# Three row norms of an attention block, moved from ScalarE to VectorE

## The reference

```python
def layer_norm(x, w, b):
    mu = mean(x); var = mean(square(x - mu))
    return (x - mu) * rsqrt(var + 1e-5) * w + b

# mod = silu(c) @ wmod, cut into sa, ca, ga, sb, cb, gb
h = _layernorm(x) * (1 + ca) + sa
# attention block on h
a  = layer_norm(h, ln1_w, ln1_b)               # the row norm "xa"
x1 = h + softmax_band(a @ Wq, a @ Wk) @ (a @ Wv) @ Wo + bo
n2 = layer_norm(x1, ln2_w, ln2_b)              # the row norm "nrm_b"
y  = x1 + gelu(n2 @ W1 + b1) @ W2 + b2
x2 = x + ga * y
h3 = _layernorm(x2) * (1 + cb) + sb            # its row norm is "nrm_c"
xr, xk = mixes of h3 with h3 of the token before
out = x2 + gb * sigmoid(xr @ W_r) * (square(relu(xk @ W_k)) @ W_v)
```

## Time and profile before

| | before |
|---|---|
| median of 3 runs | 622.71 us |
| lowest and highest | 622.13, 622.75 us |
| profiled execution, its span from first to last instruction | 620.5 us |
| median less that span | 2.2 us |
| mean granted TensorE clock | 0.989 of full |
| PE, DVE, ACT, POOL busy | 92%, 65%, 72%, 61% |
| chain of work that ended last | PE 50%, ACT 17%, DVE 15%, issue 7%, POOL 7% |
| read and written in HBM | 22.31 MB, 4.49 MB |

### The profile page before, as it was taken

The page is one execution under the profiler, slowest core; times in us unless marked ns, Lnnn a source line. Parts: engine busy times, 40 slices in busy tenths (PEclk is TensorE's granted clock), DMA queues, the critical chain, the costliest instruction groups (busy, mean ns, idle before and its releaser), DMA issues.

```text
span 620.5 us, 16499 instructions
## 1 busy us (share of the span) xinstructions
PE 567.8 (92%) x6528; PEld 444.8 (72%) x6528; DVE 403.2 (65%) x830; ACT 446.9 (72%) x745; POOL 380.3 (61%) x610
## 2 busy tenths in 40 slices
PE   5889988999898999999898989899999989999996
PEld 2668757777776777677667767677767768878785
DVE  4676746686464788576867686578867475375453
ACT  2527447499968777897879786987788798955542
POOL 4387324657937957675767678586657378943430
PEclk9989989899999999999999999999999999999999
DMA  5635423434503051351235132533134242110111
GB/s 176 246 103 133 124 77 78 112 75 116 137 18 101 25 139 52 97 143 56 69 90 153 60 87 76 146 93 89 52 80 112 70 116 52 54 46 26 34 44 35
DMA packets 46364, 55.74 MB, mean 90 GB/s; under 512 B 11643, under 2 KB 33469, under 8 KB 46286
## 3 DMA queue, kind: packets, MB, share of 16 engines
q1 hardware_dynamic: 44454, 53.81, 31.4%
q10 hardware_dynamic: 1832, 0.87, 0.6%
HBM read 22.31 MB, written 4.49 MB: 43 GB/s over the span
## 4 chain that ended last, share of the span: by engine, by line
PE 50%; ACT 17%; DVE 15%; issue 7%; POOL 7%; DMA 1%; SPq 1%; ACTq 1%; DVEq 0%; POOLq 0%
PE rest L486 4%; PE rest L498 4%; PE rest L447 3%; PE rest L449 3%; PE rest L448 3%; DVE nmax L1530 3%; PE quad L342 3%; ACT rest L1048 3%; PE rest L361 3%; PE rest L474 3%; PE rest L239 3%; PE quad L398 2%; ACT hid_hi L1058 2%; ACT p L997 2%; DVE hid_lo L1590 2%
## 5 line engine op out<-in xcount | busy, mean ns | idle before, releaser
L2174 POOL TENSOR_SCALAR_AFFINE_SELECT p<-p 128x448 f32<-128x448 f32 x64 | 41.5, 649 | 102.8 <-ACT p L997 80.5
L1530 DVE TENSOR_REDUCE nmax<-quad 128x8 f32<-128x1032 f32 x64 | 79.0, 1234 | 2.2
L430 PE MATMUL rest<-bt_hi,w_hi 128*128 128x256 f16 x256 | 70.2, 274 | 5.3 <-DVE hid_lo L1590 5.1
L997 ACT ACTIVATE p<-quad,scale_s 128x576 f32<-128x576 f32 (+1 forms) x77 | 62.3, 822 | 15.7 <-PE quad L342 15.4
L1048 ACT ACTIVATE rest<-rest,bias,scale_g 128x256 f32<-128x256 f32 x128 | 63.0, 532 | 11.2 <-PE rest L432 11.0
L447 PE MATMUL rest<-w_hi,hid_hi 128*128 128x256 f16 x256 | 69.9, 273 | 0.9 <-DVE hid_lo L1590 0.9
L432 PE MATMUL rest<-bt_hi,w_lo 128*128 128x256 f16 x256 | 69.8, 273 | 0.0
L431 PE MATMUL rest<-bt_lo,w_hi 128*128 128x256 f16 x256 | 69.8, 273 | 0.0
L449 PE MATMUL rest<-w_hi,hid_lo 128*128 128x256 f16 x256 | 69.8, 272 | 0.0
L448 PE MATMUL rest<-w_lo,hid_hi 128*128 128x256 f16 x256 | 69.8, 272 | 0.0
L1590 DVE SCALAR_TENSOR_TENSOR hid_lo<-rest,inv_f,hid_hi 128x512 f16<-128x512 f32 x64 | 46.8, 744 | 25.1 <-ACT hid_hi L1058 24.8
(11 more groups left out here) (239 smaller groups left out, 1531.9 us busy)
## 6 DMA issues: line engine op xcount, KB each, us to landing
k_st<-k_two SPq DMA_DIRECT2D x64, 128.0 KB, 2.5
v_blk<-vn SPq DMA_DIRECT2D x16, 512.0 KB, 6.4
q_st<-q_two SPq DMA_DIRECT2D x64, 64.0 KB, 2.6
k_st<-k_two SPq DMA_DIRECT2D x64, 64.0 KB, 2.0
rb<-den_rows SPq DMA_DIRECT2D x16, 256.0 KB
x<-x SPq DMA_DIRECT2D x16, 256.0 KB, 3.0
out<-x SPq DMA_DIRECT2D x16, 256.0 KB, 2.2
xa<-x SPq DMA_DIRECT2D x7, 512.0 KB, 4.8
```

Source lines behind the costliest of these rows:

```text
L430: e.matmul(dst, w1_hi[:, k, ms], bt_hi[:, k, :], start=(k == 0), stop=False)
L997: e.activation(p32[gp % SLOTS][:, c0:c0 + 2 * w].rearrange("p (n c) -> p n c", n=2), (rest if gp < APART else quad)[:, b0 % HQ:b0 % HQ + 2 ...
L1530: e.tensor_reduce(nmax[:, :, :, qt].rearrange("p a j -> p j a"), quad[:, :, 2 * QB - 2:2 * WIN].rearrange("p j (c a) -> p j a c", a=2), AX ...
```

## The change

The three norms are computed on VectorE as (x - mean) * rs, in one `tensor_scalar` per tile with mean and rs as per-row scalars. ScalarE's 96 activations (32 each for xa, nrm_b, nrm_c) go, and on GpSimd the two nb instructions of each `rstd_h`, `rstd_b`, `rstd_c` (80 in all) with the wait between them. As mean and variance are now read later, the next statistics of each kind also hold for the ve step of the ones before, ve_x holds for h2, and two waits of the start-up are added. In VectorE's list the norms stand where ScalarE ran them by the clock. The loops of the lists are written out with literal numbers; TensorE's and SyncE's instructions stay in their order.

```diff
-            def norm_a(n):                                  (ScalarE)
...
-                e.wait_ge(s_nbh, n + 1)
-                for t in range(NT):
-                    e.activation(xa[:, t, :], h[n % 3][:, t, :], ACT.Identity, bias=nb_h[:, t:t + 1],
-                                 scale=rs_h[:, t:t + 1]).then_inc(s_xa, 1)
...
             def stats_h(n):                                 (VectorE)
...
+                hold(e, s_hve, n)
                 stats(h[n % 3], st_h, mv_h, range(NT), s_hst, s_hmv, 4 * n)
+
+            def norm_a(n):
+                if not batch(n):
+                    return
+                e.wait_ge(s_hrs, n + 1)
+                for t in range(NT):
+                    e.tensor_scalar(xa[:, t, :], h[n % 3][:, t, :], mv_h[:, t, 0:1], rs_h[:, t:t + 1],
+                                    ALU.subtract, ALU.mult).then_inc(s_xa, 1)
...
+            def norm_b(i):
...
+                e.wait_ge(s_brs, i + 1)
+                hold(e, s_tr2, i)
+                for t in range(2):
+                    e.tensor_scalar(nrm_b[:, t, :], x1[:, 2 * (i % 2) + t, :], mv_b[:, t, 0:1], rs_b[:, t:t + 1],
+                                    ALU.subtract, ALU.mult).then_inc(s_n2, 1)
...
             def rstd_h(n):                                  (GpSimd; rstd_b and rstd_c likewise)
...
                 hold(e, s_xa, 4 * n)
-                e.tensor_scalar(nb_h[:, :], mv_h[:, :, 0], -1.0, None, ALU.mult)
                 e.tensor_scalar(ve_h[:, :], mv_h[:, :, 1], 1.0, EPS, ALU.mult, ALU.add).then_inc(s_hve, 1)
                 e.wait_ge(s_hve, n + 1)
                 e.tensor_tensor(rs_h[:, :], ve_h[:, :], mhalf[:, :], ALU.pow).then_inc(s_hrs, 1)
-                e.wait_ge(s_hrs, n + 1)
-                e.tensor_tensor(nb_h[:, :], nb_h[:, :], rs_h[:, :], ALU.mult).then_inc(s_nbh, 1)
```

More of the change, by code:

```diff
@@ L769, in _ @@
             transposes_d(1)
[L770 to L829, removed]
@@ new lines, in _ @@
+            values_b(1)
+            up(3, 0, 1)
+            maxima(7, 0)
+            up(3, 1, 2)
+            maxima(7, 1)
+            up(3, 2, 3)
+            up(3, 3, 4)
+            out_project(4)
+            maxima(7, 2)
+            down(3, 0)
+            scores(26, 2, 4)
+            transposes_d(2)
+            scores(27, 0, 2)
+            transposes_a(4)
+            down(3, 1)
+            maxima(7, 3)
+            keys(2)
+            scores(27, 2, 4)
+            max_rows(7)
+            project(8)
@@ new lines, in _ @@
+            up(5, 0, 1)
+            maxima(9, 0)
+            up(5, 1, 2)
+            maxima(9, 1)
+            up(5, 2, 3)
+            up(5, 3, 4)
+            out_project(6)
+            maxima(9, 2)
+            down(5, 0)
+            scores(34, 2, 4)
+            transposes_d(4)
+            scores(35, 0, 2)
+            transposes_a(5)
+            down(5, 1)
+            maxima(9, 3)
+            keys(4)
+            scores(35, 2, 4)
+            max_rows(9)
+            project(10)
+            context(8)
@@ new lines, in _ @@
+            maxima(11, 0)
+            up(7, 1, 2)
+            maxima(11, 1)
+            up(7, 2, 3)
+            up(7, 3, 4)
+            out_project(8)
+            maxima(11, 2)
+            down(7, 0)
+            scores(42, 2, 4)
+            transposes_d(6)
+            scores(43, 0, 2)
+            transposes_a(6)
+            down(7, 1)
+            maxima(11, 3)
+            keys(6)
+            scores(43, 2, 4)
+            max_rows(11)
+            project(12)
+            context(10)
@@ L1059, in high_f @@
                                  scale=inv_f[:, 1:2]).then_inc(s_hh, 1)
-            def norm_c(i):
-                if not half_batch(i):
-                    return
-                e.wait_ge(s_nbc, i + 1)
-                hold(e, s_tr3, i)
-                for t in range(2):
-                    e.activation(nrm_c[:, t, :], x2[:, 2 * (i % 2) + t, :], ACT.Identity, bias=nb_c[:, t:t + 1],
-                                 scale=rs_c[:, t:t + 1]).then_inc(s_n3, 1)
             def modulate(i):
@@ L1612, in residual_b, with norm_c @@
                 e.wait_ge(s_x2, i + 1)
+                hold(e, s_cve, i)
                 stats(x2, st_c, mv_c, range(2 * (i % 2), 2 * (i % 2) + 2), s_cst, s_cmv, 2 * i)
+            def norm_c(i):
+                if not half_batch(i):
+                    return
+                e.wait_ge(s_crs, i + 1)
+                hold(e, s_tr3, i)
+                for t in range(2):
+                    e.tensor_scalar(nrm_c[:, t, :], x2[:, 2 * (i % 2) + t, :], mv_c[:, t, 0:1], rs_c[:, t:t + 1],
+                                    ALU.subtract, ALU.mult).then_inc(s_n3, 1)
             def mix(i):
@@ L2008, in _ @@
             gated(8)
-            maxima(NU - 2, 2)
+            maxima(14, 2)
             output(8)
@@ L2556, in load_residual @@
                 hold(e, s_out, DMA * (i - 1))
+                if i == 0:
+                    hold(e, s_top, DMA)
                 if i == 1:
```

1579 lines of the change are left out of this document (1046 added, 533 removed).

## The result

The changed kernel takes 656.42 us (median of 4 runs, 655.05 to 657.33), beside 622.73 for the kernel before on the same chip. The ratio is 1.0539 with a 95% interval of 1.0519 to 1.0559: 33.7 us slower. The forecast was slower by 11.5, 634.2, in a range of 626.5 to 643. The sign was right, the size a third of what came.

What follows compares the result with a forecast made beforehand. TensorE was taken as the bound, waiting for VectorE and not ScalarE; 5.4 + 3.2 + 1.8 - 1.0 + 1.6 + 1.4 - 0.85 = +11.5 us made the span 632.0 and the time 634.2, range 626.5 to 643.

Steps and rivals of the forecast that it cites:

- the price of one: One norm on VectorE: 0.34 us, from the same operation reading PSUM; a group of two 0.7, of four 1.4.
- The port rival: Steady norm groups on VectorE collide with GpSimd over the shared port pair: some +8 us more, 642; chance 0.19.
- (a): Four xa norms between ct and the second hid_lo, four steady batches: all 1.36 us reach TensorE's out projection, +5.4.
- (b): nrm_c's norm between two hid_lo, five times: no slack before the scores that need nmax's banks, +3.2 us.
- (c): nrm_b's norm behind the four mixed, four times: 0.68 us each less 0.22 slack before the scores, +1.8.
- the groups at nothing: Each batch's other nrm_b and nrm_c, where VectorE idles before a predicated copy: 0, uncovered up to 0.7 us each.
- (d): ScalarE's relief ahead of the second hid_lo's gelu: TensorE waits less for x, 0.25 us per batch, -1.0 for four.
- (e): The first nrm_b now stands behind k_two on VectorE, so TensorE's transposes start 1.6 us later: +1.6.
- (f): xa of batch 3, directly ahead of the predicated copy whose nmax TensorE awaits: +1.4 us; other early groups 0.
- (g): The tail: the last norm's bare chain gets shorter without the two nb steps, -0.85 us; the one before gains nothing.

Runs made afterwards that it cites:

- e10: Changed kernel with all norms left out but those of the first batch and half batch, and two unread nb_b steps back on GpSimd: 623.1 us.
- e3: Changed kernel with xa and nrm_b back on ScalarE with their nb steps, only nrm_c on VectorE: 629.2 us, ratio 1.011.
- e1: Changed kernel with nrm_b and nrm_c back on ScalarE with their nb steps, only xa's norm on VectorE: 636.2 us, ratio 1.021.
- e2: Changed kernel with xa and nrm_c back on ScalarE with their nb steps, only nrm_b on VectorE: 635.5 us, ratio 1.021.
- e12: Kernel before, with only the odd half batches' nrm_b moved to VectorE: 630.5 us, ratio 1.011.
- e9: Changed kernel with the two nb_b steps put back on GpSimd, their result unread: 652.0 us, ratio 1.046.
- e11: Changed kernel with each norm also writing a row sum (accum_out) and two unread nb_b steps back on GpSimd; output no longer the norm: 642.5 us.
- e7: Kernel before, with only the last two half batches' nrm_c (4 norms) moved to VectorE: 622.4 us, ratio 0.999.
- e13: Only xa's norms on VectorE, in batches 4 to 7 moved from between ct and hid_lo to behind the last row maxima: 642.6 us, ratio 1.033.

## Why the prediction was right and wrong

**The direction, and the views.** That ScalarE "is not the one that TensorE waits for" held: taking 51 us from ScalarE gave some 1.2 in TensorE's waits and nothing that the time shows (e10), and the norms on VectorE cost TensorE new waits for nmax and hid_lo.

**The step that failed is the price of one.** "I take 0.34, the nearest: a group of two costs 0.7 (0.36 to 1.5) and a group of four 1.4 (0.7 to 3.0)." The nearest row came out of PSUM and was undisturbed. Undisturbed the norm costs 0.32, so the estimate of its own length was right. But in the steady batches GpSimd is at work for 0.70 of the time, and the groups took 2.35 to 2.6 (xa), 1.3 to 2.0 (nrm_b) and 0.8 to 1.6 (nrm_c). The port rival had the mechanism and a chance of 0.19, and took a contended group for 0.67 or 1.34 more; it too priced only groups on the path. Its 642 was 14 short.

**(a)** 5.4 was forecast, e1's steady part is 9.7 longer, 8.1 of them in the wait for hid_lo. That nearly all of the group reaches TensorE was right (2.0 of 2.3 us), its length was wrong, and so was the way: the up product's wait for hid_lo, not the out projection's.

**(b), (c) and the groups at nothing.** 5.0 was forecast for both, e2 and e3 show 16.9 in the steady part. The length again; then the cover: the odd nrm_b's 0.65 us of idle time would have hidden nearly all of 0.68 and did not hide 2.0 (2.7, e12); then S, which no term had: GpSimd's lost steps were costed as a gain in the tail and nothing else, and are a loss, 3.0 us of waits in the steady part and 3 to 5 in the medians (e9 to e11).

**(d)** -1.0 was forecast for ScalarE's relief. TensorE's wait for x fell by 1.2 (e3, e10), so the term and its path were right.

**(e)** TensorE waited 1.30 for the first nrm_b, 1.6 forecast:

```profile
125.21 0.66 PE L411 MATMUL rest<-ident,nrm_b 128*128 128x128 f32 x4 [1.30 <-DVE nrm_b L1856]
```

**(f)** The wait behind xa of batch 3 grew by 1.16, 1.4 forecast; it was 0.42. "The other early groups lie in gaps or beside warm matmuls: 0" was wrong. The start is 7.2 longer, at the same busy time of TensorE (206.2 us, before 206.0), and (e) and (f) make 2.5 of it. TensorE's waits for nmax there grew by 4.4 in all, (f) among them, and those for hid_lo by 2.0, while xa of one early batch took 2.85 and four groups of two 1.45 to 2.03. The wait of (f) now:

```profile
159.12 0.76 PE L342 MATMUL quad<-q_st,k_st 100*128 100x192 f16 x9 [1.58 <-DVE nmax L1808]
```

**(g)** -0.85 was forecast, and the chain is 0.93 shorter; yet the changed kernel's end is 0.9 longer, since nrm_b and nrm_c meet GpSimd there as well (0.85 to 1.7 us for two). In e7 the end is 0.6 shorter.

**What the 33.7 us are.** Without the port's waits and with the shift mended, but at 0.46 us for a norm, 19.6 remain (e11). The prediction's own sum, done again at 0.46, gives 16.6 (an estimate), so the paths that it named carry most of that. e9 less e11 is 9.6: the port's waits, less the 0.14 us by which each of e11's norms is longer. The shift is 4.4 by the medians (changed less e9).

Where the steady part's 25.7 us are lost the trace shows, the kernel before above, the changed one below:

```profile
231.40:498.90 267.50, 250.88 (x3012) 192.29 (x3012) 187.11 (x370) 218.12 (x366) 181.65 (x290) 1.00 0.34 91
238.60:531.80 293.20, 256.85 (x3012) 193.76 (x3012) 218.81 (x418) 194.41 (x318) 175.80 (x251) 0.99 0.31 83
```

TensorE idles 19.7 us more and is busy for 6.0 more. The idle time is, by its waits: +8.4 for hid_lo ahead of the up product, +7.0 for nmax ahead of the scores, +2.4 for nmax at L252, +2.3 for mixed, +1.1 for hid_lo ahead of the down product, -1.2 for x, -0.4 ahead of the out projection. About half of the busy time goes with two short stretches at half the clock, at 243.8 and 390.5 us: TensorE is busy for 65.1 and 65.0 us in the batches that hold them, for 63.4 and 63.3 in the other two. Before there are none. Each begins 1.3 us or less after a wait of over 2 us for hid_lo has ended, as the two of e9 and the one of e1 do after theirs of 2.0. So part of the lost clock comes with the long waits; that it comes from them was not tested. The changed kernel's four runs had 0.981 to 0.986 of the clock. The 25 runs of the kernel before on one chip had 0.984 to 0.997, 0.991 in the mean, and there a clock lower by 0.007 goes with some 3 us, an estimate from a line through them. Some 3 of the 33.7 us are of this kind.

## What to carry to other kernels

Before work goes to VectorE, ask of the new instruction not only how long it is, but whom it excludes: here one that waits for no semaphore took over three times its length when it met GpSimd. Look in the trace of before for the rows whose maximum is far above their median (mixed, 1212 against 480 ns), and at what GpSimd does at the time; those are the instructions that a shift of either engine by 0.3 us or so lengthens or spares. An idle gap covers a group only at the group's length under disturbance, and removing work from an engine off the path is an edit of the timing, with either sign.

## What the runs showed of the hardware

- A tensor_scalar of 128x256 fp32 within SBUF takes 0.40 us, 0.32 from start to start, and up to 1.39 when it meets a GpSimd instruction; with 2 columns 0.28, and 1.04 when it does.
- With a sum written out it takes 0.53, 0.46 from start to start, its read 0.08 beside the next, and never more than 0.54.
- Instructions with two inputs in SBUF stretch too (median 480 and maximum 1212 ns for mixed before, 682 and 1475 for the residual sum). The statistics, with one input (392 to 428 ns in all 32 of st_b), and hid_lo, with one of two in PSUM (716 to 752), did not.
- GpSimd's own steps of 2 columns did not hold mixed up (1.67 us beside them), though the pow takes 0.8 us.
- In the steady parts TensorE's clock fell to half for a short stretch only right behind a wait of some 2 us (six times: 2.28 and 2.04 in the changed kernel, 1.98 in e1, 2.01 and 2.06 in e9, 2.26 in e13); eight other waits of that length were followed by no fall.
